# A Mamba block with a binarised feed-forward, batch by batch: where norms, second output products and chunk steps stand in each engine's order

## What is computed

```python
def _layernorm(x, axis=-1, eps=1e-05):
    m = jnp.mean(x, axis=axis, keepdims=True)
    v = jnp.var(x, axis=axis, keepdims=True)
    return (x - m) / jnp.sqrt(v + eps)
...
x = input_tensor @ Wx.T;  z = input_tensor @ Wz.T
x = jax.nn.silu(_causal_conv(x, conv_w, conv_b))          # 4 taps
b = (x @ Wb.T);  c = (x @ Wc.T)                           # 8 heads, state 64
dt = jax.nn.softplus(x @ Wdt.T + b_dt);  a = -jnp.exp(log_a)
y = _ssd_scan(xh, b, c, dt, a) + d_param * xh             # state = exp(dt a) state + dt b x, y = c state
yn = (y - mean) / sqrt(var + EPS) * gn_w + gn_b           # over all tokens and the head's 64 channels
attn = (yn * jax.nn.silu(z)) @ Wout.T
...
ffn = gelu(x @ bw1.T + b1) @ bw2.T + b2                   # bw = mean|w| * sign(w), rows of w1 and w2
...
x = x + _layernorm(attn(_layernorm(x)))
x = x + _layernorm(ffn(_layernorm(x)))
```

## Time and profile before

| what | value |
|---|---|
| median of 3 runs | 1361.92 us (1361.39 to 1361.99) |
| the profiled execution's own time | 1363.99 us |
| its span | 1362.2 us |
| mean granted PE clock of the span | 0.98 of full |
| PE / DVE / ACT / POOL busy | 1253.5 / 1039.2 / 831.6 / 458.4 us |
| matmuls | 10744 |
| HBM traffic | 23 GB/s over the span |

### The profile page before, as it was taken

The page is one execution under the profiler, slowest core; times in us unless marked ns, Lnnn a source line. Parts: engine busy times, 40 slices in busy tenths (PEclk is TensorE's granted clock), DMA queues, the critical chain, the costliest instruction groups (busy, mean ns, idle before and its releaser), DMA issues.

```text
span 1362.2 us, 28268 instructions
## 1 busy us (share of the span) xinstructions
PE 1253.5 (92%) x10744; PEld 800.6 (59%) x10744; DVE 1039.2 (76%) x2432; ACT 831.6 (61%) x1432; POOL 458.4 (34%) x527
## 2 busy tenths in 40 slices
PE   6999899999999999999998999999999999989675
PEld 3564657566565756656575665757556475756543
DVE  4664787878879797878978787796977788787574
ACT  5664675657755585656856577565856568565433
POOL 2030433323351334315333243513343153332533
PEclk9998999999999999999999999999999999999888
DMA  7010000101000010100101010010101000000000
GB/s 221 1 48 1 17 0 2 47 1 48 1 18 32 2 47 1 48 1 17 32 2 47 1 48 0 3 47 2 47 2 48 1 2 32 2 32 1 32 1 31
DMA packets 30565, 32.91 MB, mean 24 GB/s; under 512 B 1856, under 2 KB 28628, under 8 KB 30432
## 3 DMA queue, kind: packets, MB, share of 16 engines
q1 hardware_dynamic: 30432, 31.11, 7.1%
HBM read 22.72 MB, written 8.39 MB: 23 GB/s over the span
## 4 chain that ended last, share of the span: by engine, by line
PE 49%; DVE 19%; issue 14%; POOL 12%; ACT 5%; POOLq 0%; DVEq 0%; ACTq 0%
PE bank L1490 21%; PE bank L1675 8%; PE bank L1660 4%; PE bank L1688 4%; DVE xs L1125 4%; POOL Cd L814 3%; PE bank L1602 2%; POOL xdw L807 2%; DVE un L1097 2%; PE bank L1580 2%; DVE hh L1304 2%; DVE gn_stats L1261 1%; POOL state L825 1%; PE bank L1529 1%; POOL y L777 1%
## 5 line engine op out<-in xcount | busy, mean ns | idle before, releaser
L814 POOL TENSOR_TENSOR Cd<-Cd,CT 128x512 f32<-128x512 f32 x64 | 81.2, 1269 | 360.5 <-ACT Cd L1033 360.0
L1490 PE MATMUL bank<-sh,WbT 128*128 128x512 f16 x768 | 177.8, 385 | 12.4 <-DVE sh L1130 12.4
L1490 PE MATMUL bank<-sh,WcT 128*128 128x512 f16 x768 | 175.9, 379 | 0.0
L1490 PEld LDWEIGHTS bank<-sh,WbT 128*128 128x128 f16 x768 | 72.9, 99 | 103.7 <-DVE sh L1130 22.1
L1125 DVE SCALAR_TENSOR_TENSOR xs<-xi,vectors,xs 128x512 f32<-128x512 f32 x168 | 125.2, 749 | 4.5 <-ACT xs L938 0.8
L1490 PEld LDWEIGHTS bank<-sh,WcT 128*128 128x128 f16 x768 | 75.1, 98 | 86.6
L1675 PE MATMUL bank<-uh,sign1T 128*128 128x512 f16 x512 | 121.8, 383 | 2.5 <-DVE uh L1332 2.5
L1062 ACT ACTIVATE hf<-bank,vectors,alpha 128x512 f32<-128x512 f32 x128 | 99.6, 778 | 39.2 <-PE bank L1675 28.0
L1688 PE MATMUL bank<-sign2T,hh 128*128 128x256 f16 x1024 | 119.0, 275 | 1.8 <-DVE hh L1345 1.8
L999 ACT ACTIVATE CT<-bank 128x512 f32<-128x512 f32 x64 | 38.1, 595 | 134.1 <-PE bank L1490 134.1
L1688 PEld LDWEIGHTS bank<-sign2T,hh 128*128 128x128 f16 x1024 | 99.6, 99 | 19.0 <-issue 4.3
(11 more groups left out here) (207 smaller groups left out, 2682.4 us busy)
## 6 DMA issues: line engine op xcount, KB each, us to landing
xt<-L_attn_input_tensor_dram SPq DMA_DIRECT2D x16, 512.0 KB, 5.0
u<-L_attn_input_tensor_dram SPq DMA_DIRECT2D x16, 512.0 KB, 4.0
out_dram<-u SPq DMA_DIRECT2D x16, 512.0 KB, 3.0
yT<-in_L_ffn_w_dram SPq DMA_DIRECT2D x2, 512.0 KB, 9.6
u<-in_L_ffn_w_dram SPq DMA_DIRECT2D x2, 512.0 KB, 9.5
BT<-in_L_attn_Wx_dram SPq DMA_DIRECT2D x1, 512.0 KB, 4.8
BT<-in_L_attn_Wz_dram SPq DMA_DIRECT2D x1, 512.0 KB, 5.7
zs<-in_L_attn_Wb_dram SPq DMA_DIRECT2D x1, 512.0 KB, 5.6
```

The lines of the kernel that those rows point to most:

```text
L814: pool.tensor_tensor(Cd[n % 2][:, :, :], Cd[n % 2][:, :, :], CT[:, :, q * P:(q + 1) * P], ALU.mult)\
L1490: mm = nc.tensor.matmul(bank(t, key)[:, :], w[i][:, k, cols(m)], v[h][:, k, :], start=(a == 0), stop=(a == len(terms) - 1))
```

## The change

1. In the tail's feed-forward, both `O` products stand together, before `score` 0; before, the second stood after `carry` 0.
2. The end norm's steps stand earlier: statistics and root after `back` 0 (before: after `back` 1), the norm itself after `back` 1 (before: after `carry` 2).
3. In the chunk stage `ends` q stands before `front` q; the turned inputs `xT` before `back` of the same chunk; the next input norm's statistics after `H` 1, the norm before `O`; the first half's head statistics of pair 0 in the C stage of half 1.
4. The shifts of the input, end and now also the feed-forward norm are made by POOL as a product of `minus_mean` (a new row on DVE) and the root. The feed-forward norm is applied by ACT, no longer by DVE. The very first input norm is applied by DVE.
5. A place is left out (`None`) in the own ring before the last `carry` of half 1.

The core of the diff:

```diff
@@ class Ring
+            if key is None:
+                continue
@@ turn_steps
-        steps += own(("C", j, 0), ("cums", j)) + tail(("uT", j)) + own(("roles", j), ("skip", j), ("C", j, 1)) + tail(("H", j, 0), ("H", j, 1))
+        steps += own(("C", j, 0), ("cums", j)) + tail(("uT", j)) + own(("roles", j), ("skip", j), ("C", j, 1))
+        steps += tail(("H", j, 0), ("H", j, 1)) + [(who, "in_stat", nj)]
...
-        steps += own(("C", j, 2)) + tail(("H", j, 2), ("H", j, 3))
+        steps += own(("C", j, 2)) + tail(("H", j, 2), ("H", j, 3)) + (own(("head_stat", 0, 0)) if j else [])
...
-        steps += own(("decays", j), ("ends", j, 0), ("front", j, 0)) + [(who, "in_stat", nj)] + tail(("O", j, 0))
+        norm, xT = [(who, "in_norm", nj)], [[(who, "xT", nj, k)] for k in range(KD)]
+        steps += own(("decays", j), ("ends", j, 0), ("front", j, 0)) + ([] if first else norm) + tail(("O", j, 0), ("O", j, 1))
...
-        steps += own(("score", j, 0), ("front", j, 1))
+        steps += own(("score", j, 0), ("ends", j, 1), ("front", j, 1))
...
-        steps += own(("score", j, 1))
-        norm = [(who, "in_norm", nj)]
-        steps += own(("carry", j, 0), ("ends", j, 1)) + (own(("back", j, 0)) + norm if first else norm + tail(("O", j, 1)) + own(("back", j, 0)))
-        steps += own(("front", j, 2)) + [(who, "xT", nj, 0)] + own(("score", j, 2), ("carry", j, 1), ("ends", j, 2))
-        steps += [(who, "xT", nj, 1)] + own(("back", j, 1)) + tail(("end_stat", j)) + own(("front", j, 3), ("score", j, 3)) + tail(("end_root", j))
+        steps += own(("score", j, 1), ("carry", j, 0)) + ([] if first else xT[0]) + own(("back", j, 0)) + tail(("end_stat", j), ("end_root", j))
+        steps += (norm if first else []) + own(("ends", j, 2), ("front", j, 2)) + (xT[0] if first else [])
+        steps += own(("score", j, 2), ("carry", j, 1)) + xT[1] + own(("back", j, 1)) + tail(("end_norm", j, 0), ("end_norm", j, 1))
+        steps += own(("ends", j, 3), ("front", j, 3), ("score", j, 3))
...
-        steps += own(("carry", j, 2), ("ends", j, 3)) + tail(("end_norm", j, 0), ("end_norm", j, 1)) + own(("back", j, 2))
+        steps += own(("carry", j, 2), ("back", j, 2))
...
-        steps += [(who, "silu_table")] + own(("carry", j, 3), ("back", j, 3)) + ([] if j else own(("head_stat", 0, 0)))
+        steps += [(who, "silu_table")] + own(("carry", j, 3), ("back", j, 3))
@@ own ring's keys
+            if (who, kind, *at) == ("own", "carry", NJ - 1, NQ - 1):
+                own_keys.append(None)
@@ POOL, inverse_root
+                    if w in ln_shift:
+                        pool.wait_ge(*ln_rstd[w].count(t, j + 1))
+                        pool.tensor_tensor(ln_shift[w][:, :], minus_mean[w][:, :], rstd[w][:, :], ALU.mult)\
+                            .then_inc(ln_shifts[w].sem, 1)
@@ ACT
+            def ff_norm(t, j):
+                for i in range(NQ):
+                    normal("ff", un, u[j], t, j, i)
@@ DVE, statistics
                 if w in normed:
                     dve.wait_ge(*normed[w].count(t, j * NQ))
+                    nc.vector.tensor_scalar(minus_mean[w][:, :], moments[w][:, :, 0], -1.0, None, ALU.mult)
@@ DVE
-            def shift(w):
...
-            def ff_norm(t, j):
-
-                for i in range(NQ):
-                    normal("ff", t, j, un[:, i, :], u[j][:, i, :], i).then_inc(un_out.sem, 1)
```

More of the change, by code:

```diff
@@ L95, in __init__ @@
     def __init__(self, tensors, full_sems, keys, once, freed=None):
-        self.tensors, self.full_sems, self.keys, self.once, self.freed = tensors, full_sems, keys, once, freed
+        self.tensors, self.full_sems, self.once, self.freed = tensors, full_sems, once, freed
+        self.keys = [key for key in keys if key is not None]
         self.place, self.each = {}, [0] * len(tensors)
@@ L354, in mamba_sandwich_kernel @@
         rstd = {w: sb(f"rstd_{w}", [P, NQ]) for w in LNS}
-        ln_shift = {w: sb(f"ln_shift_{w}", [P, NQ]) for w in ("in", "end")}
+        ln_shift = {w: sb(f"ln_shift_{w}", [P, NQ]) for w in ("in", "ff", "end")}
+        minus_mean = {w: sb(f"minus_mean_{w}", [P, NQ]) for w in ln_shift}
         gn_stats = sb("gn_stats", [P, KI, NJ * 2, 6])
@@ L482, in mamba_sandwich_kernel @@
         ln_rstd = {w: Signal(sem(f"ln_rstd_{w}"), NJ) for w in LNS}
-        ln_shifts = {w: Signal(sem(f"ln_shifts_{w}"), NJ) for w in ("in", "end")}
+        ln_shifts = {w: Signal(sem(f"ln_shifts_{w}"), NJ) for w in ln_shift}
         xn_made = Signal(sem("xn_made"), NJ * NQ)
@@ L540, in mamba_sandwich_kernel @@
         o_out = Signal(sem("o_out"), NJ * NQ)
-        normed = {"in": xn_made, "end": y2_norm}
+        normed = {"in": xn_made, "ff": un_out, "end": y2_norm}
         def ffn_buffer(t, j):
@@ L890, in table, with normal @@
                 return lambda t: nc.scalar.activation(table_in[:, :], ones[:, 0:1], func)
-            def normal(w, v, t, j, i):
+            def normal(w, out, v, t, j, i):
                 act.wait_ge(*ln_shifts[w].count(t, j + 1))
-                nc.scalar.activation(v[:, i, :], v[:, i, :], ACT.Identity, bias=ln_shift[w][:, i:i + 1],
+                nc.scalar.activation(out[:, i, :], v[:, i, :], ACT.Identity, bias=ln_shift[w][:, i:i + 1],
                                      scale=rstd[w][:, i:i + 1]).then_inc(normed[w].sem, 1)
             def input_norm(t, j):
+                for i in range(0 if opening(t) else NQ):
+                    normal("in", xt[j], xt[j], t, j, i)
+            def ff_norm(t, j):
                 for i in range(NQ):
-                    normal("in", xt[j], t, j, i)
+                    normal("ff", un, u[j], t, j, i)
             def end_norm(t, j, m=None):
                 for i in range(NQ) if m is None else range(2 * m, 2 * m + 2):
-                    normal("end", ffn_buffer(t, j), t, j, i)
+                    normal("end", ffn_buffer(t, j), ffn_buffer(t, j), t, j, i)
             def input_high(t, j, k):
@@ L1102, in input_stats, with input_norm @@
                            lambda i: dve.wait_ge(*x_in[j].count(t, 1)) if i == 0 else None)
-            def shift(w):
-                def step(t, j, m=0):
-                    if m:
-                        return
-                    dve.wait_ge(*ln_rstd[w].count(t, j + 1))
-                    nc.vector.scalar_tensor_tensor(out=ln_shift[w][:, :], in0=moments[w][:, :, 0], scalar=-1.0,
-                                                   in1=rstd[w][:, :], op0=ALU.mult, op1=ALU.mult).then_inc(ln_shifts[w].sem, 1)
-                return step
+            def input_norm(t, j):
+                for i in range(NQ if opening(t) else 0):
+                    normal("in", t, j, xt[j][:, i, :], xt[j][:, i, :], i).then_inc(xn_made.sem, 1)
             def input_low(t, j, k):
```

16 lines of the change are left out of this document (8 added, 8 removed).

## The result

The changed kernel takes **1393.64 us** (median of 4 runs, 1392.98 to 1397.26), the kernel before, on the same chip, 1361.95 us (1361.39 to 1362.65): ratio 1.0238, 95% interval 1.0219 to 1.0256. It is slower by 32 us where 35 were forecast. The profiled execution took 1397.26 us, with a span of 1395.3.

A forecast was written before the change was run, and what follows sets the result against it. TensorE's stream (busy 92%) plus its waits was taken as the bound. Terms gave +5.35 us a turn, times 7 +37.5, with edges +36: 1398 on the median, stated as 1397 us, range 1385 to 1412 (chance 0.62).

The forecast's parts named there:

- Part 1: Half 0, feed-forward norm moved to ACT ahead of eight head normalisations: first H product starts later, +2.9 us a turn.
- The clock: After the 3.2 us TensorE wait at half 0's first H, the clock falls in 6 of 7 turns, +1.6 us each.
- Rival (a): Stalls smaller than laid out: clock unharmed (-9.4 us), chunk stages even (-13.7), giving 1375 us; chance 0.17.
- Part 2: Half 1, feed-forward norm on ACT with no head normalisations behind it: turning of `un` ends later, +0.85 us a turn.
- Part 3: Chunk stages, with O products together and end statistics and root earlier: +0.35 us in half 0, +1.6 in half 1.
- three laid-out waits: Chunk stage, half 0: TensorE waits 0.55 us through xdt's bank, 1.35 for the state, 0.65 for yT; sum 2.55.
- Rival (b): Faster: chunk stages lose all waits, -3 us a turn, 1341 us, if POOL's scaling of state 1 begins early; chance 0.09.
- Part 4: Projection stage of half 1: TensorE's waits of 0.43, 0.80 and 0.49 us vanish, -1.7 us a turn, taken as the most.
- Part 5: Edges: opening up to -1 us, closing tail sheds 1.38 us of `un` on DVE but pays in half 0; together -1.5.
- One sign: Profile after the change: PE idle near 11 us a turn instead of 7.2.

The follow-up runs named there:

- number 1: The change, but in half 0 ACT's eight head normalisations stand ahead of the four feed-forward norms; 1364.35 us, 1.0009 of the kernel before.
- number 7: The change without the bank place it leaves out before the last carry of half 1; 1392.93 us, 1.0212 of the kernel before.
- number 3: The kernel before with only the norms of the change (shifts on POOL, feed-forward norm on ACT), its step order and banks untouched; 1379.8 us, 1.0124.
- number 11: number 1 with the end root and its shift behind POOL's scaling of the state, and the end norm behind carry 2; 1328.81 us, 0.9751 of the kernel before.
- number 4: The kernel before with only the change's order of steps, norms and bank ring as before; 1436.68 us, 1.0543.
- number 5: number 4 with the end norm itself back behind carry 2, its statistics and root still a chunk sooner; 1368.48 us, 1.0041 of the kernel before.
- number 6: The change with the feed-forward norm back on DVE, the input and end norm shifts still on POOL; 1368.88 us, 1.0044 of the kernel before.
- number 8: number 3 with the eight head normalisations ahead of the feed-forward norm on ACT; 1344.41 us, 0.9863 of the kernel before.

## Why the prediction was right

**Part 1** named the cause, and it is shown: number 1 takes it away and 29 us go. Its term was 2.9 us, found 2.59. The start of ACT's `un` (13.0 us into the turn, found 12.9) and the POOL product, the one unknown price, 0.2 between bounds of 0.10 and 1.02, came out as laid out.

**The clock.** Six falls of seven were forecast at 1.57 us each, 9.4 us in all; six came, and H to the first E took 11.3 us more over the seven turns. The price was near; the count is in part luck, since number 7 has the same seven waits of 3.02 us and three falls. Rival (a), of which an unharmed clock was a part, falls. The Trainium skill's page "TensorE: Matmul & The Clock Gate", Part 1, has the throttled state as the default that activity releases. The rows agree in kind: at each of these falls the products resume at the lower level. By that rule alone I would have had seven falls here; behind the same 3.02 us there were six, seven in number 3 and three in number 7.

**Part 2** was 0.85, found 0.63. **Part 3** was +0.35 and +1.6, found +0.47 and +1.59. Two of its three laid-out waits held (state 1.35, found 1.18; yT 0.65, found 0.54); that for xdt was 0.55 and is 0.23. The scaling of state 1 was to end at +23.1 and ended at +23.1 (561.04, with the first E at 537.92). The recorded waits came to 1.95 us and not 2.55, less than the 2.19 of before, and the stage still grew as forecast: a recorded wait is not all that TensorE loses at it, and the sum had no term for that. So the number is better than its parts. Rival (b) said that the stage decides at POOL, by when the scaling begins; that was the right place. It came 2.92 us behind its request here, and in number 11, where it comes 1.02 behind, the gain is of the kind that (b) described, by the opposite move: (b) had the root early enough, number 11 has it behind the scaling. My layout had Cd behind the late variance, and I took that for given.

**Part 4** was -1.7 as the most that TensorE's own waits could give back; it is -2.24. The cap failed because TensorE loses more at a wait than is recorded: the three waits come to 1.72 us, and the stage, with the same products and none of the waits, is 2.24 shorter. Which part of the change brings it I had wrong: number 3 shows 1.8 of it with the order of before.

**Part 5 and the sum.** The edges were -1.5. The opening is better by 5.1 us, where I had up to 1: the first dt product comes 1.8 us sooner and the one of the next batch another 3.3. The last turn and the closing tail are 6.4 us longer, where the sum had 4.9. Between the first and the last turn the six turns grew by 31.7 us, 5.3 each, as the sum had it (5.35), but unevenly: four by 3.1 to 4.7, the last two by 7.9 and 7.5. In these two the fall at the first H cost 3.0 and 2.9 us, and the clock fell once more, at 970 and 1137 us, at the end of a chunk stage, for 1.6 us. So the parts of the turn read come to 4.35, 1.0 below the forecast, and low grants that I had not in the sum make up for it. That the mean turn meets the sum so closely is luck; the cause and its order of size are not. Spans differ by 33.1 us, medians by 32, and the sum had 36.

**One sign failed.** PE was to be idle near 11 us a turn; it is 8.6 (163.86 less 155.28 busy), against 7.5 before. Of the 4.35 us by which the turn grew, the profile shows 1.1 as idle time and 3.25 as busy time; 1.3 of that is the lower clock, the rest is not shown as a wait.

**What the prediction had no way to show** is that its parts do not add. It costed the order's steps as if the norms did not matter to them. Order alone costs 74 us, norms alone 17, both 32: the shifts on POOL are what makes the early end norm bearable (numbers 4 to 7), and the head normalisations behind `un` are what makes the norms dear (numbers 1, 3, 8).

## What to carry to other kernels

In an engine that works in order, a step that has to wait costs twice: its own time, and everything ready behind it. Look at each moved instruction's operand as well as its length: a root of 1.02 us that stood ahead of three POOL operations instead of behind them cost 1.9 us a half. A version whose time agrees with another's need not agree in cause: numbers 5 and 6 took the same time by different turns. Before a change of engine or order is given up, move what stands behind it: three steps moved in the list turned +32 us into -34. And undo parts in both directions, alone and together, since here one half of the change was worse than the whole.
